# Second attention layer: four heads at a time in groups of 32 rows and columns of TensorE, the bias multiplied separately, each consumer one step behind its producer

## The reference

```
q, k, v = x @ Wq.T + bq, x @ Wk.T + bk, x @ Wv.T + bv     # each 256 x 128, then seen as 16 heads x 256 positions x 8
att = softmax(q @ k.T)                                     # per head, 256 x 256, no scale
att_out = (att + rel_bias[buckets]) @ v                    # the bias is added AFTER the softmax
a = layer_normalize(att_out @ Wo.T + bo + x)
out = layer_normalize((a @ W1.T + b1) @ W2.T + b2 + a)
```

## Time and profile before

| what | us |
|---|---|
| runs of the kernel before | 1712.19, 1718.55, 1726.85; median 1718.55 |
| the profiled execution | 1728.99, with a span of 1727.2 |
| layer 0, both parts | up to 1164.5 |
| layer 1 attention: start to first scores | 39.7 |
| layer 1 attention: first to last scores | 394.7 |
| layer 1 attention: last scores to the barrier | 50.6 |
| layer 1 experts | 77.7 |

### The profile page before, as it was taken

One profiled execution on the slowest core, in us unless ns is written; L12 is line 12 of the kernel. 1 busy time (PEld: TensorE's weight loads), 2 busy tenths in 40 slices (PEclk: granted clock), 3 DMA queues, 4 the chain that ended last, 5 costly groups with the idle time before them and its releaser, 6 DMA issues. The chain is left out here.

```text
span 1727.2 us, 31707 instructions
## 1 busy us (share of the span) xinstructions
PE 1357.6 (79%) x8972; PEld 1081.3 (63%) x8972; DVE 1095.3 (63%) x2565; ACT 941.2 (54%) x2748; POOL 817.2 (47%) x824
## 2 busy tenths in 40 slices
PE   2267887878798956988998988985898989999452
PEld 0044565555565746988997988971676666676352
DVE  3575788787877527447447456431678887888512
ACT  1155675665676825666666666652566545655110
POOL 2446647637566113655664655653434353432103
PEclk6588998899988967999999999996889878989576
DMA  6300000000000005020020000006111101220064
GB/s 209 110 2 2 1 9 3 7 9 2 6 8 2 8 13 212 10 109 11 10 112 8 10 10 11 12 10 200 26 32 32 25 25 24 34 31 10 13 195 113
DMA packets 127182, 72.27 MB, mean 42 GB/s; under 512 B 78297, under 2 KB 118489, under 8 KB 126681
## 3 DMA queue, kind: packets, MB, share of 16 engines
q1 hardware_dynamic: 116664, 60.95, 12.4%
q0 software_dynamic: 3200, 6.56, 1.5%
q10 hardware_dynamic: 7200, 3.41, 0.7%
HBM read 53.26 MB, written 17.12 MB: 41 GB/s over the span
## 5 line engine op out<-in xcount | busy, mean ns | idle before, releaser
L1438 POOL TENSOR_TENSOR hl<-hid,hh 128x256 fp32r<-128x256 f32 x396 | 293.7, 744 | 221.2 <-ACT hh L1415 217.4
L1481 DVE SCALAR_TENSOR_TENSOR hid<-GU,gub,sg 128x256 f32<-128x256 f32 x396 | 190.6, 482 | 194.8 <-ACT sg L1409 115.1
L1309 PE MATMUL GU<-xh,wh 128*128 128x256 f32 x792 | 233.3, 295 | 40.4 <-DVE wl L1457 31.2
L1409 ACT ACTIVATE sg<-GU,gub 128x256 f32<-128x256 f32 x396 | 188.1, 475 | 123.6 <-PE GU L1311 121.5
L1311 PE MATMUL GU<-xh,wl 128*128 128x256 f32 x792 | 225.7, 285 | 0.0
L1310 PE MATMUL GU<-xl,wh 128*128 128x256 f32 x792 | 225.6, 285 | 0.0
L1845 ACT ACTIVATE prob<-S,negmax 128x256 f32<-128x256 f32 x256 | 119.2, 470 | 168.8 <-DVE negmax L2230 164.1
L1309 PEld LDWEIGHTS GU<-xh,wh 128*128 128x128 f32 x792 | 152.2, 192 | 49.9 <-issue 28.0
L1415 ACT CAST hh<-hid 128x256 fp32r<-128x256 f32 x396 | 158.2, 399 | 26.5 <-DVE hid L1481 25.4
L1721 PE MATMUL S<-kpad,qn 128*128 128x512 f32 x256 | 155.0, 691 | 1.5 <-POOL kpad L1965 1.4
L1310 PEld LDWEIGHTS GU<-xl,wh 128*128 128x128 f32 x792 | 152.6, 193 | 0.0
(11 more groups left out here) (290 smaller groups left out, 3251.0 us busy)
## 6 DMA issues: line engine op xcount, KB each, us to landing
raw<-in_expert_w SPq DMA_DIRECT2D x4, 2688.0 KB, 12.1
modb<-mod_d SPq DMA_DIRECT2D x2, 2688.0 KB, 15.5
list<-zero SPq DMA_DIRECT2D x5, 1024.0 KB, 9.6
raw<-in_expert_w SPq DMA_DIRECT2D x4, 1152.0 KB, 6.4
wa<-in_w SPq DMA_DIRECT2D x16, 256.0 KB, 3.9
wb<-in_w SPq DMA_DIRECT2D x16, 256.0 KB, 4.7
kpad<-rel_d SPq DMA_DIRECT2D x1, 3072.0 KB, 14.3
qkv_d<-qkvT SPq DMA_DIRECT2D x24, 128.0 KB, 4.6
```

The lines of the kernel that those rows point to most:

```text
L1309: pe.matmul(out, lhs[0], rhs[0], start=start, stop=False, skip_group_check=True)
L1409: act.activation(sg[:, c % BUFS], GU[c % BUFS][:, 0:TT], ACT.Silu, bias=gub[:, GATE, e * CH0 + c:e * CH0 + c + 1]).then_inc(silu, 1)
L1438: pool.tensor_tensor(hl[:, b], hid[:, b], hh[:, b].bitcast(F32), ALU.subtract).then_inc(hid_lo, 1)
L1481: dve.scalar_tensor_tensor(out=hid[:, c % BUFS], in0=GU[c % BUFS][:, TT:2 * TT], scalar=gub[:, UP, e * CH0 + c:e * CH0 + c + 1], in1=sg[:, ...
```

## The change

`layer1_attention` is written anew; the other functions change only in that layer 0's set-up semaphores become one. The program is now a list of steps, -22 to 93, eight to a row, all unrolled. Work with offset o of row b runs at step 8b + o, and offsets are chosen so that an engine takes up what another made in the step before.

- **Layout.** A head now has 32 rows of SBUF: 8 with its values, a ninth for the maximum, the rest zero (`QA`, `KA`). Four heads stand under each other, four such quads make a row. Keys, queries and values are projected by token (two matmuls 384 wide), VectorE adds the bias, and 6 + 8 + 1 transfers carry them through DRAM.
- **Scores, twice.** At step i the scores of two heads (128 queries by 256 keys, two blocks) are made only for their maxima; four steps later the transposed scores (keys by queries) of two heads are made with the maximum already added to the queries' ninth row, so that the exponential of the result is the transposed probability, not yet divided. In one step the two kinds alternate, and the four matmuls of a block stand in four different row groups.
- **Maximum.** VectorE reduces all 1024 columns of S in one instruction; TensorE transposes the maxima of a quad, VectorE adds them to `QA`.
- **AV in two steps.** Per quad, eight matmuls with 32 weight columns multiply values with the bias (`bias_values`) and, a step later, eight multiply them with the exponentials (`values`); the ninth value column is ones and gives the sum. ScalarE copies both halves of O out at once. 8 transfers write them to DRAM, 2 read them back by token, and there VectorE divides and adds (three instructions a row).
- **Gone** are `kpad`, the probability multiply-add, the 64 transposes of probabilities a row with their copies, the reordering copies, and the second buffers of the scores: S and ST each fill two banks and have one buffer.
- **Moved.** The mixing of the expert outputs goes from VectorE to GpSimd (`mix_outputs`, four instructions a row); GpSimd's first gather now waits for the weight loads (six), and SyncE starts the big loads without waiting for the gather.

```diff
+STEPS = 8
+FIRST_STEP, LAST_STEP = -22, STEPS * (NB - 1) + 37
+def row_at(step, offset):
+    row, off = divmod(step - offset, STEPS)
+    return row if off == 0 and 0 <= row < NB else None
...
-        kpad = sb("kpad", [P, 2, H1, NT])
-        prob = sb("prob1", [P, 4, 2, NT])
-        qkvT = sb("qkvT", [P, 3, NT])
+        QA = sb("QA", [P, 2, QUADS, NT])
+        KA = sb("KA", [P, 2, QUADS, NT])
+        V = sb("V_1", [P, 2, 2, H1, BLOCK])
+        OE = sb("OE", [P, 2, QUADS, 512])
...
-        PT = ps("PT_1", [P, 2, 512])
-        O = [ps(f"O_1{k}", [P, 512]) for k in range(2)]
+        ST = ps("ST_1", [P, 2, 512])
+        O = ps("O_1", [P, 512])
+        NM = ps("NM_1", [P, 512])
+        bankE = Turns(sem("te_full"), sem("te_drained"), {"hT": -10.5, "qkv0": -9.5, "qkv1": -7.5, "vT": 3.5, "router": 33.5, "pos": 36.5})
+        bankL = Turns(sem("tl_full"), sem("tl_drained"), {"oT": 20.5, "wo": 21.5, "aT": 24.5, "uT": 25.5, "w2": 26.5})
+        bankN = Turns(sem("nm_full"), sem("nm_drained"), {"top0": 2, "top1": 4, "top2": 6, "top3": 8, "h2T": 31.5})
...
+            def step_program(step):
+                b = row_at(step, -7)
+                if b is not None:
+                    bankE.wait_emptied(sp, "qkv1", b)
+                    of = io["qkv_d"][b].rearrange("(k d) (l c) -> l k d c", d=ROWS, c=16)
+                    for t in range(TILES):
+                        for k in range(3):
+                            sp.dma_start(of[t * P:(t + 1) * P, k, 0:DH1],
+                                         qkv[:, t, k * D:(k + 1) * D].rearrange("p (d c) -> p d c", c=16)).then_inc(qkv_out, 16)
+                    sp.wait_ge(qkv_out, 96 * (b + 1))
+                    if b >= 2:
+                        sp.wait_ge(t_mm, STEPS * (b - 1))
+                    for k, to in ((K_, KA), (Q_, QA)):
+                        for j in range(4):
+                            sp.dma_start(to[32 * j:32 * j + ROWS, b % 2],
+                                         io["qkv_d"][b, k * ROWS:(k + 1) * ROWS].rearrange("d (g j x) -> d g j x", j=4, x=NT)[:, :, j]).then_inc(qk_in, 16)
+                    bankE.wait_full(sp, "vT", b - 1)
+                    sp.dma_start(vT[:], io["qkv_d"][b, V_ * ROWS:V_ * ROWS + DH1].rearrange("d (h x) -> (d h) x", x=NT)).then_inc(v_in, 16)
+                b = row_at(step, 15)
+                if b is not None:
+                    sp.wait_ge(o_out, QUADS * (b + 1))
+                    of = io["o_d"][b].rearrange("(o d) (g j x) -> d g j o x", d=ROWS, j=4, x=NT)
+                    for j in range(4):
+                        for o in range(2):
+                            sp.dma_start(of[:, :, j, o], OE[32 * j:32 * j + ROWS, b % 2, :, o * NT:(o + 1) * NT]).then_inc(o_sent, 16)
+                    sp.wait_ge(o_sent, 128 * (b + 1))
+                    if b >= 1:
+                        sp.wait_ge(dO, NO * b)
+                    for t in range(TILES):
+                        sp.dma_start(ol[:, t], io["o_d"][b].rearrange("s (t l c) -> t l s c", t=TILES, c=16)[t]).then_inc(o_in, 16)
...
+            def scores(step):
+                s, t = halves_at(step)
+                if s:
+                    row, i = s
+                    if i == 0:
+                        pe.wait_ge(qk_in, 128 * (row + 1))
+                        if row == 0:
+                            pe.wait_ge(B_out, B_STEPS)
+                    if STEPS * row + i > 0:
+                        pe.wait_ge(s_max, STEPS * row + i)
+                if t:
+                    row, i = t
+                    if i % 2 == 0:
+                        bankN.wait_emptied(pe, f"top{i // 2}", row)
+                    if STEPS * row + i > 0:
+                        pe.wait_ge(t_exp, STEPS * row + i)
+                for blk in range(2):
+                    for e in range(2):
+                        if s:
+                            row, i = s
+                            j, g = 2 * (i % 2) + e, i // 2
+                            mm = pe.matmul(S[:, e, blk * NT:(blk + 1) * NT], QA[32 * j:32 * j + BLOCK, row % 2, g, blk * P:(blk + 1) * P],
+                                           KA[32 * j:32 * j + BLOCK, row % 2, g, :], start=True, stop=True)
+                            if blk == 1 and e == 1:
+                                mm.then_inc(s_mm, 1)
+                    for e in range(2):
+                        if t:
+                            row, i = t
+                            j, g = 2 * (1 - i % 2) + e, i // 2
+                            mm = pe.matmul(ST[:, e, blk * NT:(blk + 1) * NT], KA[32 * j:32 * j + BLOCK, row % 2, g, blk * P:(blk + 1) * P],
+                                           QA[32 * j:32 * j + BLOCK, row % 2, g, :], start=True, stop=True)
+                            if blk == 1 and e == 1:
+                                mm.then_inc(t_mm, 1)
+            def tops(row, quad):
+                pe.wait_ge(s_max, STEPS * row + 2 * quad + 2)
+                bankN.wait_drained(pe, f"top{quad}", row)
+                for q in range(2):
+                    mm = pe.transpose(NM[:, q * P:(q + 1) * P], top_now[:, quad % 2, q, :], ident)
+                mm.then_inc(bankN.full, 1)
+            def bias_values(row, quad):
+                if quad == 0:
+                    bankE.wait_emptied(pe, "vT", row)
+                if QUADS * row + quad > 0:
+                    pe.wait_ge(o_out, QUADS * row + quad)
+                for kb in range(2):
+                    for j in range(4):
+                        head = 4 * quad + j
+                        pe.matmul(O[32 * j:32 * j + BLOCK, NT:2 * NT], V[:, row % 2, kb, head, :],
+                                  B[:, head, P * (1 - kb):P * (1 - kb) + NT], start=(kb == 0), stop=(kb == 1), skip_group_check=True)
+            def values(row, quad):
+                pe.wait_ge(t_exp, STEPS * row + 2 * quad + 2)
+                for kb in range(2):
+                    for j in range(4):
+                        mm = pe.matmul(O[32 * j:32 * j + BLOCK, 0:NT], V[:, row % 2, kb, 4 * quad + j, :],
+                                       pT[:, quad % 2, j, kb, :], start=(kb == 0), stop=(kb == 1), skip_group_check=True)
                 mm.then_inc(o_mm, 1)
...
+                now = quad_at(step, 8)
+                if now:
+                    row, quad = now
+                    act.wait_ge(o_mm, QUADS * row + quad + 1)
+                    if row >= 2 and quad == 0:
+                        act.wait_ge(o_sent, 128 * (row - 1))
+                    act.copy(OE[:, row % 2, quad, :], O[:]).then_inc(o_out, 1)
+                b = row_at(step, 4)
...
+                if t:
+                    row, i = t
+                    act.wait_ge(t_mm, STEPS * row + i + 1)
+                    done = QUADS * row + i // 2 - 1
+                    if i % 2 == 0 and done > 0:
+                        act.wait_ge(o_mm, done)
+                    first = 2 * (1 - i % 2)
+                    act.activation(pT[:, (i // 2) % 2, first:first + 2].rearrange("p j k q -> p (j k q)"),
+                                   ST[:].rearrange("p e x -> p (e x)"), ACT.Exp).then_inc(t_exp, 1)
...
+            pool.wait_ge(w_in, 16 * n_w)
...
+            def mix_outputs(b):
...
+            def maxima(row, i):
+                dve.wait_ge(s_mm, STEPS * row + i + 1)
+                quad = i // 2
+                if i % 2 == 0 and QUADS * row + quad >= 2:
+                    before = QUADS * row + quad - 2
+                    bankN.wait_full(dve, f"top{before % QUADS}", before // QUADS)
+                first = 2 * (i % 2)
+                to = top_now[:, quad % 2].rearrange("p q (j c) -> p j q c", j=4)[:, first:first + 2, :, DH1]
+                dve.tensor_reduce(to, S[:].rearrange("p e (q k) -> p e q k", q=2), X, ALU.max, negate=True).then_inc(s_max, 1)
+            def tops(row, quad):
+                bankN.wait_full(dve, f"top{quad}", row)
+                of = QA[:, row % 2, quad, :]
+                dve.tensor_tensor(of, of, NM[:, 0:NT], ALU.add).then_inc(bankN.drained, 1)
...
+            def add_bias(b, t):
+                bankE.wait_full(dve, f"qkv{t}", b)
+                if t == 0 and b >= 1:
+                    dve.wait_ge(qkv_out, 96 * b)
+                dve.tensor_tensor(qkv[:, t, :], TE[:, 0:3 * D], b3[:], ALU.add).then_inc(bankE.drained, 1)
...
+            at_e = {-15: (1, 2, 3), -12: (4, 5, 6), -10: (7,)}
+            at_a = {19: (1, 2, 3), 22: (4, 5, 6), 23: (7, 8), 27: (9, 10, 11), 28: (12, 13, 14)}
+            at_b = {29: (1, 2, 3), 30: (4, 5, 6), 34: (7, 8, 9, 10, 11), 35: (12, 13, 14, 15), 37: range(16, 29)}
...
```

More of the change, by code:

```diff
@@ L1546, in slot_is, with wait_drained, wait_full @@
-def slot_is(slot, n):
-    return isinstance(slot, int) and slot == n
+        uses = sorted((STEPS * row + at, name, row) for name, at in stages.items() for row in range(NB))
+        self.place = {(name, row): i for i, (_, name, row) in enumerate(uses)}
+    def wait_drained(self, eng, name, row):
```

(86 more changed lines are left out.)

705 lines of the change are left out of this document (252 added, 453 removed).

## The result

The changed kernel takes 1617.57 us in the median of four runs (1616.6 to 1626.53), the kernel before 1719.12 on the same chip; the ratio is 0.9413, with an interval from 0.9381 to 0.9444. The forecast was 1600, in 1550 to 1680. In the profiled executions the span went from 1727.2 to 1614.8, and the attention stage from 485.0 to 369.6, where 366 was forecast. That agreement is luck in part: two terms were off by more than 20 us each, in opposite directions, the first by TensorE's clock and the second by it in part. Of the remaining 14 us between 1600 and 1617.6, 10.4 are the amount by which the median lay under the profiled execution before; here the profiled one, 1616.6, is itself the lowest of the four.

The account below looks back on a forecast made before the run. The prediction took TensorE and VectorE, both nearly full, to bound the kernel. The attention stage, 46 + 255 + 65 = 366 against 485.0 us, was 119 less: 1610 profiled, 1600 as median, range 1550 to 1680.

Parts of the forecast that it names:

- Scores and AV: TensorE's step: eight 256-column score matmuls over four row groups in 1.1 us, AV's sixteen records in 1.1 us.
- The heads: Attention stage from first to last scores, 64 steps: 53 + 36 + 166, together 255 us.
- The ring without a clock loss: Single-buffered scores and maximum wait for each other: about 33 us a full row, 4.1 a step at 2.4 GHz.
- So full rows will alternate: I take 38 us, 4.75 a step: Steps 29 to 63: clock alternates between levels, 4.75 us a step between 4.1 and 5.25, 166 us in all.
- The end: Stretch behind the last scores: 12 + 3 + 12 + 38, 65 us (56 to 70).
- four more transposed steps, 12: First term behind the last scores: four steps with transposed scores, 12 us.
- the chain: Last term behind the last scores: division and output projection as before, 38 us.
- Transfers: SyncE's 25 issues a row take 26 us, under 38, hidden; uncovered, O costs DVE 1 to 3 us a row.
- Hidden: GpSimd loses 16 x 0.845 us a row and gains four mixing instructions, some 4: hidden unless landing on a power function.
- All at 2.4 GHz: Rival: full clock throughout, stage 42 + 226 + 58 = 326 us, kernel 1560; chance 0.15.
- Slower: row groups only in pairs, at the low clock: Rival at `scores`: pairs at 1.2 GHz, 6.9 us a step, 440 for the heads, kernel 1785; chance 0.06.
- the rival on the low clock: Rival: low clock throughout, PE never full enough; stage 58 + 319 + 70 = 447 us, kernel 1681; chance 0.15.

Follow-up runs that it names:

- turned behind AV: The changed kernel with the four transposed score matmuls of a step issued behind AV instead of beside the four score matmuls: 1824.52 us, ratio to before 1.0617.
- scores apart: The changed kernel with a step's four score matmuls queued first and the four transposed ones behind them, instead of in turns: 1615.16 us.
- Older rows first: The changed kernel with VectorE taking the older row's work first within a step, and TensorE the older row's positions before the younger one's transposes: 1609.36 us.
- Tail filled: The changed kernel with row 7's score matmuls repeated in steps 64 to 67 and 22 unread 512-column matmuls from step 71 on: 1615.09 us.

## Why the prediction was right, and where it was not

**Scores and AV.** Right: four row groups at once, 1.15 for eight (1.1 said), AV 1.07 (1.1). The sum of 8 x 0.43 over the measured 1.15 is 3.0. The 3.07 of the Trainium skill, TensorE: Matmul & The Clock Gate, Part 3, agrees with it; the 0.26 us a step that I had worked out from that figure did not come on top, since my 1.1 held start and drain already.

**The heads, 255 said, 233.6 measured.** By its parts, from maximum to maximum: the first 19 steps 60.8 (53 said), the next ten 34.5 (36), the last 34 gaps 139.8, or 4.11 a step. The ring without a clock loss was worked out at 4.1, and rows 5 and 6 take 32.7 and 32.2 where it gave 33; row 4, with 37.4, is longer than the ring explains. The failed step is the one on the clock, "So full rows will alternate: I take 38 us, 4.75 a step": 35 x 0.65 = 23 us too much. I had taken the 2.28 busy of 3.40 us ahead of one fall as the sign of every fall. Between the first scores and the last the clock is low only for 17.1 us in row 0, where it falls while the scores still run without the transposed ones, and for four patches of 3.4 or 6.8 us. Row 5 has 0.97 with TensorE busy 79% of the time, outside the 0.6 to 0.9 that I had named as a sign, and turned behind AV 0.50 with 98%. The first 19 steps were too cheap in the forecast, in part by those 17.1 us.

**The end, 65 said, 88.3 measured.** The failed step is the first term, "four more transposed steps, 12", with 3 for the last AV: 30.0 us. In these steps the four ST stand alone, TensorE also has rows 5 and 6 to serve, and at the low level that fills it, 27.5 of 30.0. I had costed the tail at the full clock. Where the clock held, as in scores apart, the same work took 10 less; the other 5 are not taken apart. The trip of O was right (12 said, 13.2), and the chain is 44.4 for 38. The trace shows at least a part of why: VectorE finishes rows 5 and 6 inside it, behind its wait for row 7.

```profile
1477.88 6.48 SPq L1686 DMA_DIRECT2D o_d<-OE  x8
...
1486.20 1.85 SPq L1693 DMA_DIRECT2D ol<-o_d  x2
1491.07 0.35 DVE L2090 RECIPROCAL rZ<-ol 128x32 f32<-128x32 f32 x1 [5.62 <-DMA ol<-o_d]
...
1493.80 0.16 DVE L2170 TENSOR_TENSOR hot<-const,topf 128x32 f32<-128x32 f32 x1
...
1500.12 0.42 DVE L2099 TENSOR_TENSOR r<-TL,hk 128x256 f32<-128x256 f32 x1
```

`hot` here is row 5's; row 7's output projection is done at 1497.59 and taken up at 1500.12, 9 us after its reciprocal, when VectorE has no wait left. Older rows first left this work inside the chain and only reordered it, which is why its 0.7 us does not price it.

**The start.** 47.65 for 46, by the gathers as said: the first mixing at 20.0 us.

**Transfers.** Right: SyncE's 25 issues of a row take some 19 us in row 5, 24.8 from the first one's start to the last one's end with the waits between, where 26 was said, and VectorE has no wait for O in the heads.

**GpSimd.** "Hidden" left something out: mixing there slows VectorE beside it, by some 0.9 us a row.

**The rivals.** "All at 2.4 GHz" gave 226 for the heads and was nearer there than the forecast; its 58 for the end was not. "Slower: row groups only in pairs, at the low clock" did not happen, but turned behind AV is that case built: 440 for the heads said, 437.1 measured, 1785 said, 1824.5 measured. What stood against the rival on the low clock, "at 1.2 GHz PE is full, and then the clock came back", does not hold in that run: TensorE is full there and the clock does not come back for 457 us. The 0.06 was too low for it, too, since "both must hold" took pairs and the low clock as two separate accidents, and in that run they come together. One slip of numbers: the low-clock rival's 1681 lies just outside the range to 1680 that is said to take it in.

## What to carry to other kernels

Fill all four row groups, and put no instruction of another form between those that are to run side by side; their order among themselves made no difference here. Do not take a nearly always busy TensorE as a sign of the full clock: price a stretch in which fewer groups run together at the low level too. And look at a pipeline's drain as a stretch of its own, where the youngest row queues behind older ones on engines that work in order. A lag of one step between producer and consumer is cheap in the middle and is paid once at the end.

## What was not expected of the hardware

TensorE at a busy share of 98% (60.58 of 61.93 us) was granted 0.50 for 457 us, with half of its row groups idle during scores and a fourfold column form for AV. The Trainium skill, TensorE: Matmul & The Clock Gate, Part 1, ties the clock to how busy the engine has been; this run does not fit that. Whether the idle rows are the reason, or the changes of form between the groups, no run separates. Tail filled does not separate them either: its matmuls over the whole array brought 0.75 for 0.50, and took away idle time as well.
